# Longitude synthesis moved, by row block, into the prologue of the spiking stage; the spiking weights prepared in the stage of the synthesis over degrees

## The reference

```python
x = x + _L0_conv_ref(_ln_c(x), L0_conv_w1r, L0_conv_w1i, L0_conv_w2r, L0_conv_w2i)   # spherical harmonics: analysis, mixing, synthesis
t = _to_tokens(x)
t = t + _L0_ffn_ref(_ln_t(t))             # decodes nibbles, shifts, adds one-hot rows
x = _from_tokens(t, x)
x = x + _L1_conv_ref(_ln_c(x), ...)       # spiking attention, 8 heads, time axis = batch
t = _to_tokens(x)
t = t + _L1_ffn_ref(_ln_t(t), ...)        # two of eight experts for each token
```

```python
def _isht(c):
    g = jnp.einsum('lmj,bclm->bcjm', P_SYN, c) * (1.0 / np.sqrt(TWO_PI))   # over degrees l
    return jnp.fft.irfft(g, n=NLON, axis=-1) * NLON                        # over orders m: "longitude"
```

## Time and profile before

| | us |
|---|---|
| median of 3 runs | 1368.16 (1367.49 to 1375.95) |
| the profiled execution | 1366.96 |
| its span, first to last instruction | 1364.5 |
| synthesis block | 203.1 to 283.5 |
| weights' block | 283.5 to 299.1 |
| prologue, to the first projection | 299.1 to 334.5 |
| spiking loop, from its first sign | 345.8 to 877.4 |
| experts | from 877.4 |

### The profile page before, as it was taken

How to read it: one execution, slowest core, us unless ns; L and a number is a source line. 1 busy time by engine, 2 the same in 40 slices (tenths; PEclk the granted TensorE clock), 3 DMA queues, 4 the chain that set the end, 5 groups by cost and what they waited for, 6 DMA issues and landing times. The chain is left out here.

```text
span 1364.5 us, 23969 instructions
## 1 busy us (share of the span) xinstructions
PE 993.5 (73%) x6628; PEld 845.5 (62%) x6629; DVE 857.8 (63%) x2741; ACT 655.1 (48%) x1400; POOL 573.4 (42%) x739
## 2 busy tenths in 40 slices
PE   7937665931577767676776754129999999999997
PEld 6827663721355556565565543028888888888886
DVE  6715432454557889889878454616666666666675
ACT  3427532207385887777865342114444444444443
POOL 3310000212022257566655477645555555555554
PEclk9978887875777888797867655559999999999999
DMA  9998949910001001000000000011111111111110
GB/s 277 201 236 157 210 104 261 240 43 20 19 20 49 20 19 41 15 24 23 11 26 15 28 25 27 21 51 45 42 43 46 48 48 48 45 47 48 46 37 1
DMA packets 122841, 93.08 MB, mean 68 GB/s; under 512 B 10760, under 2 KB 111476, under 8 KB 122001
## 3 DMA queue, kind: packets, MB, share of 16 engines
q1 hardware_dynamic: 103121, 66.48, 21.6%
q0 software_dynamic: 9088, 17.33, 3.9%
q10 hardware_dynamic: 10560, 8.39, 2.3%
HBM read 55.61 MB, written 38.39 MB: 69 GB/s over the span
## 5 line engine op out<-in xcount | busy, mean ns | idle before, releaser
L1663 POOL DMA_INDIRECT out_dram<-res,index x156 | 155.8, 999 | 217.7 <-DVE res L1746 192.4
L1793 ACT ACTIVATE sil<-ps_h 128x512 f32<-128x512 f32 x156 | 93.1, 597 | 254.6 <-PE ps_h L1845 254.6
L1711 DVE TENSOR_TENSOR act_rows<-ps_h,sil 128x512 f32<-128x512 f32 x156 | 108.0, 692 | 132.9 <-ACT sil L1793 132.8
L1864 PE MATMUL ps_y<-r_raw,aT 128*128 x1248 | 164.9, 275 | 0.0
L153 POOL DMA_INDIRECT slots<-x_sb,r_pos x128 | 130.9, 1023 | 54.0 <-issue 33.0
L1864 PEld LDWEIGHTS ps_y<-r_raw,aT 128*128 128x128 f32 x1248 | 151.7, 192 | 0.1
L1843 PE MATMUL ps_h<-wp,uTh 128*128 x312 | 137.5, 441 | 1.9 <-DVE uTl L1705 1.6
L1844 PE MATMUL ps_h<-wp,uTh 128*128 x312 | 124.4, 399 | 0.0
L1845 PE MATMUL ps_h<-wp,uTl 128*128 x312 | 122.8, 394 | 0.0
L1070 PE MATMUL ps_q<-wqkv,zT 128*128 128x256 f32 x256 | 114.5, 540 | 0.0
L1182 POOL TENSOR_TENSOR x_sb<-x_sb,sy 128x256 f32<-128x256 f32 x64 | 43.9, 687 | 145.6 <-ACT sy L1318 145.4
(11 more groups left out here) (233 smaller groups left out, 2482.8 us busy)
## 6 DMA issues: line engine op xcount, KB each, us to landing
slots<-zero SPq DMA_DIRECT2D x4, 2652.0 KB, 26.2
pay<-slots SPq DMA_DIRECT2D x39, 272.0 KB, 2.8
wc<-in_L_conv_w1r SPq DMA_DIRECT2D x8, 512.0 KB, 11.4
wc<-in_L_conv_w1i SPq DMA_DIRECT2D x8, 512.0 KB, 11.8
wc<-in_L_conv_w2r SPq DMA_DIRECT2D x8, 512.0 KB, 11.7
wc<-in_L_conv_w2i SPq DMA_DIRECT2D x8, 512.0 KB, 11.7
coefficients<-c ACTq DMA_DIRECT2D x4, 1024.0 KB, 8.6
coefc<-coefficients ACTq DMA_DIRECT2D x16, 256.0 KB, 6.1
```

What stands on the lines that cost most here:

```text
L1663: nc.gpsimd.indirect_dma_start(out_rows, bass.IndirectOffsetOnAxis(at, 0), res[:, m % RES, :], None, bounds_check=TOKENS - 1, oob_is_err=F ...
L1711: nc.vector.tensor_tensor(act_rows[:, k], ps_h[:, k, :, DFF:], sil[:, k], ALU.mult).then_inc(s_act, 1)
L1793: nc.scalar.activation(sil[:, k], ps_h[:, k, :, 0:DFF], ACT.Silu).then_inc(s_sil, 1)
L1864: ins = nc.tensor.matmul(dst, aT[:, k, (2 * e + h) * P:(2 * e + h + 1) * P], raw[:, 4 + h, col], start=(h == 0), stop=(h == 1))
```

## The change

The block of the longitude synthesis is gone. The synthesis over degrees stays in a block, which also does the work of the weights' block: the loads `lw` and `par` are issued behind `psyn` and ahead of `einv` and `gin`, PE turns the weights ahead of its 32 products, and DVE prepares the weights ahead of its 8 copies. The result goes to `routing.orders`, which lies in the memory that the experts' weights take later, so these are loaded only once all of it is turned (`sp.wait_ge(s_ct, 2 * NP2)`).

The longitude synthesis runs in the spiking stage's block, by row block instead of by batch: PE starts with 8 times (8 transposes, 8 products), ACT's copies and DVE's additions stand between the pieces of the prologue, and POOL's copies `hc` are dropped. The products go to two banks, `ps_o` and `ps_y`, in turn (before: four), and DVE frees each by one addition of 512 columns. The statistics of row block i wait for its additions. In ACT's program the scalings of row block 1 move from the prologue to behind the first signs, and of `z` only the first quarter stands ahead of the first projection.

```diff
@@ -142,9 +142,10 @@
     def allocate(self, sb):
 
         self.pos = sb("r_pos", [P, NTILES], U32)
-        self.raw = sb("r_raw", [P, 6, E * C])
+        kept = sb("r_raw", [P, 10, E * C])
+        self.raw, self.last = kept[:, 0:6], kept[0:C - 1, 6:10]
+        self.orders = kept[:, 0:8].rearrange("p a f -> p (a f)").rearrange("p (b h r m) -> p b h r m", b=B, h=HP, r=2)
         self.bias = sb("r_bias", [P, E * C])
-        self.last = sb("r_last_channel", [C - 1, 4, E * C])
 
     def scatter(self, nc, slots, x_sb, w, q):
 
...
-                with pe.Fori(0, B // 2) as pair:
-                    for k in range(2):
-                        b = pair * 2 + k
-
-                        def transposes(g):
-                            pe.wait_ge(s_hT, b * 2 + g + 1)
-                            for q in range(G):
-                                t0 = (g * G + q) * 2
-                                ins = nc.tensor.transpose(ps_t[:, g % 2, q * P:(q + 1) * P],
-                                                          hc[:, k, t0:t0 + 2].rearrange("p q r m -> p (q r m)"), ident[:, :])
-                            ins.then_inc(s_tr, 1)
-
-                        def grid(g):
-                            pe.wait_ge(s_hT, b * 2 + g + 3)
-                            pe.wait_ge(s_yfree, b * 2 + g + 1)
-                            for q in range(G):
-                                ins = nc.tensor.matmul(ps_y[:, g, q], hT[:, g, q * P:(q + 1) * P], einv[:, :],
-                                                       start=True, stop=True)
-                            ins.then_inc(s_y, 1)
-
-                        pe.wait_ge(s_hc, b + 1)
-                        transposes(0)
-                        transposes(1)
-                        grid(0)
-                        grid(1)
-
...
-                        pool.wait_ge(s_tr, b * 2 + 1)
-                        nc.gpsimd.tensor_copy(hc[:, k], h_sb[:, b]).then_inc(s_hc, 1)
...
-                            dve.wait_ge(s_y, n + 3)
-                            for bank in range(2):
-                                rows = x_sb[:, bass.ds(n * 2 * G + bank * G, G), 0:C]
-                                ins = nc.vector.tensor_tensor(
-                                    rows, rows, ps_y[:, g, bank * 2:bank * 2 + 2].rearrange("p q (j c) -> p (q j) c", j=2), ALU.add)
-                            ins.then_inc(s_yfree, 1)
...
         with nc.Block() as block:
             @block.sync
             def _(sp):
+                sp.dma_start(psyn[:, :, :], t["legendre_synthesis"].rearrange("p (m q) -> p m q", m=M)).then_inc(s_psyn, 16)
                 sp.dma_start(lw[:, :, :], t["L1_conv_lin_w"].rearrange("i d c -> d i c")).then_inc(s_load, 16)
                 for n, name in enumerate(("lin_b", "bn_g", "bn_b", "bn_m", "bn_v")):
                     with nc.allow_non_contiguous_dma(reason="512 parameters, once"):
                         sp.dma_start(par[:, n, :], t[f"L1_conv_{name}"].rearrange("i d -> d i")).then_inc(s_load, 16)
+                sp.dma_start(einv[:, :], t["fourier_inverse"]).then_inc(s_einv, 16)
+                for j in range(4):
+                    for op in range(2):
+                        for half in range(2):
+                            src = mixed[op].rearrange("l (j h r) f -> j h l (r f)", j=4, h=2)[j, half]
+                            p0 = op * 64 + half * L2
+                            sp.dma_start(gin[p0:p0 + L2, j].rearrange("p r m o -> p (r m o)"), src).then_inc(s_gin[j], 16)
+                sp.wait_ge(routing.s_zero, 2)
+                part = SLOT_TILES // 4
+                for n in range(4):
+                    sp.dma_start(slots.rearrange("(q p) c -> p q c", p=P)[:, n * part:(n + 1) * part, :],
+                                 routing.zero[:, :].unsqueeze(1).broadcast_to([P, part, XW])).then_inc(routing.s_clear, 16)
...
@@ -713,6 +617,15 @@
                 nc.vector.tensor_copy(wqkv[:, :], ps_w[:, 0:3 * C])
                 nc.vector.tensor_copy(bias[0:3, :], ps_b[:, :])
                 split3(nc, chain, [wo[:, n, :] for n in range(3)], ps_w[:, 3 * C:4 * C], rest[:, :])
+                for n2 in range(1, M // 2, 2):
+                    dve.wait_ge(s_leg, n2 + 1)
+                    evacuate(nc.vector.tensor_copy, n2).then_inc(s_h[1], 1)
+
+            @block.scalar
+            def _(act):
+                for n2 in range(0, M // 2, 2):
+                    act.wait_ge(s_leg, n2 + 1)
+                    evacuate(lambda o, i: nc.scalar.activation(o, i, ACT.Copy), n2).then_inc(s_h[0], 1)
 
...
@@ -722,13 +635,25 @@
                 for i in range(4):
                     ins = nc.tensor.transpose(ps_b[:, i * C:(i + 1) * C], bpart[:, i, :], ident[:, :])
                 ins.then_inc(s_t, 1)
-    return wqkv, wo, bias, ones
+                pe.wait_ge(s_psyn, 16)
+                for n in range(M):
+                    j, at = n // (M // 4), n % (M // 4)
+                    if at == 0:
+                        pe.wait_ge(s_gin[j], 16 * 4)
+                    if n % 2 == 0 and n >= 4:
+                        pe.wait_ge(s_h[(n // 2) % 2], n // 4)
+                    ins = nc.tensor.matmul(ps_g[:, (n // 2) % 2, n % 2, :], psyn[:, at * 4 + j, :],
+                                           gin[:, j, :, at, :], start=True, stop=True)
+                    if n % 2:
+                        ins.then_inc(s_leg, 1)
+    return wqkv, wo, bias, ones, einv, s_einv
...
+        def grid_bank(u):
+            return (ps_o if u % 2 == 0 else ps_y)[:, :]
...
+        def orders_turned(pe, i, g):
+
+            need(pe, s_chT, (i - 1) * 2 + g + 1)
+            for q in range(G):
+                ins = nc.tensor.transpose(ps_kv[:, g, q * P:(q + 1) * P],
+                                          h_sb[:, g * G + q, 2 * i:2 * i + 2].rearrange("p h r m -> p (h r m)"), ident[:, :])
+            ins.then_inc(s_ct, 1)
+
+        def orders_copied(act, i, g):
+
+            act.wait_ge(s_ct, i * 2 + g + 1)
+            need(act, s_cg, ((i - 1) * 2 + g) * 2 + 2)
+            nc.scalar.activation(hT[:, g, :], ps_kv[:, g, :], ACT.Copy).then_inc(s_chT, 1)
+
+        def grid(pe, i, g):
+
+            pe.wait_ge(s_chT, i * 2 + g + 1)
+            for h in range(2):
+                u = (i * 2 + g) * 2 + h
+                need(pe, s_ca, u - 1)
+                for q in range(2):
+                    at = (h * 2 + q) * P
+                    ins = nc.tensor.matmul(grid_bank(u)[:, q * 2 * C:(q + 1) * 2 * C], hT[:, g, at:at + P], einv[:, :],
+                                           start=True, stop=True)
+                ins.then_inc(s_cg, 1)
+
+        def grid_added(dve, i):
+
+            for n in range(4):
+                u = i * 4 + n
+                dve.wait_ge(s_cg, u + 1)
+                rows = xv[:, 2 * n:2 * n + 2, i]
+                nc.vector.tensor_tensor(rows, rows, grid_bank(u).rearrange("p (b j c) -> p b j c", b=2, j=2), ALU.add).then_inc(s_ca, 1)
+
         def statistics(dve, n):
 
             need(dve, s_xu, n)
+            dve.wait_ge(s_ca, n * 4 + 4)
             chain = Chain(dve, s_schain, n * LN_LINKS)
             layer_norm_stats(nc, chain, st, tmp[:, 0], tile(n), NT, 1e-5, -1.0).then_inc(s_var, 1)
...
@@ -1330,6 +1298,7 @@
                 sp.dma_start(before_f[:, :], t["token_before"]).then_inc(s_const, 16)
                 sp.dma_start(routing.bias[:, :], t["L1_ffn_b2"].rearrange("(a e) c -> a (e c)", a=1).broadcast_to([P, E * C]))\
                     .then_inc(routing.s_bias, 16)
+                sp.wait_ge(s_ct, 2 * NP2)
                 for k in range(4):
                     sp.dma_start(routing.raw[0:C - 1, k, :].rearrange("p (e f) -> p e f", e=E),
...
@@ -1346,7 +1315,9 @@
 
             @block.vector
             def _(dve):
+                grid_added(dve, 0)
                 statistics(dve, 0)
+                grid_added(dve, 1)
                 nc.vector.memset(every[:, :], 1.0)
                 nc.vector.memset(chosen[:, :, :], 0.0)
                 nc.vector.memset(fill[:, :], 0.0)
@@ -1359,11 +1330,17 @@
                 dve.wait_ge(s_const, 128)
                 nc.vector.tensor_copy(before[:, :], before_f[:, :]).then_inc(s_set, 1)
                 dve.wait_ge(s_set, 1)
+                grid_added(dve, 2)
+                grid_added(dve, 3)
                 ffn_flags(dve, 0)
+                grid_added(dve, 4)
                 ffn_value(dve, 0)
                 ffn_shift(dve, 0)
+                grid_added(dve, 5)
+                grid_added(dve, 6)
                 ffn_add(dve, 0)
                 z_statistics(dve, 0)
+                grid_added(dve, 7)
                 statistics(dve, 1)
 
                 def beside(i, b):
@@ -1455,13 +1432,27 @@
 
             @block.scalar
             def _(act):
-                u_rows(act, 0, 0, NT)
-                x_rows(act, 0, 0, NT)
-                for g in range(G):
+                def copied(i):
+
+                    for g in range(2):
```

(45 more changed lines are left out.)

108 lines of the change are left out of this document (17 added, 91 removed).

## The result

Before took 1368.5 us (median of 20 runs, 1358.7 to 1385.5), the changed kernel 1348.8 us (20 runs, 1338.1 to 1364.8). The ratio is 0.9841, with a 95% interval of 0.9814 to 0.9869: 21.8 us of 1368.5. Some executions of either kernel are over 1.5% slower than its fastest; the medians are over all runs, the ratios leave these out.

A forecast was written before the change was run, and what follows sets the result against it. Bound: the dependent chain to the loop's first sign, and SP's clearing issue holding the barrier. Sign 20.9 us earlier, 2.0 given back: 1366.96 - 18.9 = 1348.1, with 1.2 for the median 1349 us; range 1343 to 1355.

The forecast's parts named there:

- The barrier, 55.7 us behind `psyn`: End of the merged stage over degrees: SP's clearing issued at 258.6, spiking stage starts at 258.9 us instead of 299.1.
- the third rival: Stage over degrees: SP does not hold the barrier, so it ends at 242.7, 16 us earlier: 1333 us; chance 0.06.
- The first block added after 9.5 us: Start of the merged prologue: cold PE takes 1.97 us for transposes and 6.10 for products, then copies and last addition.
- The chain through DVE from there to POOL's start on the z statistics, 42.2 us: Merged prologue: statistics, row blocks, cast, flags, value and shift in turn on DVE, from 9.5 to 51.7 us.
- The tail, 12.0 us: Prologue's end: POOL 3.6, z rows 1.6, PE's turn 1.1, `zT` 0.6, hand-overs 0.9, projection 4.2; sign at 63.7 us.
- The allowance of 2.3 us for a dip of the clock: Merged prologue: PE's clock could drop between steps while waiting for DVE; half a block's slowdown added, giving 66 us.
- 2.0 us back in the first steps: Behind the first sign: ACT's moved rows hidden in the first step, lengthening the next two by 0.95 us each.
- `before_f` covered by 2.7 us: Spiking stage's constants: landing at 274.6 us behind the clearing, while DVE asks for them at 277.3.
- The second rival: Spiking stage's constants come late, 26.2 us from issue to landing; DVE waits 11.3 us: 1360 us; chance 0.09.
- Loop and experts as long as before; `r_raw` free: Behind the prologue: loop and experts keep their length; `r_raw`, loaded from about 305 us, isn't needed before 877: zero cost.
- The fourth rival: Spiking loop: steps fall to PE's lower clock, a mean of 0.65 costing 47.7 us: 1397 us; chance 0.06.
- the first rival: Merged prologue: PE stays at the lower clock, blocks about 9 us each, sign at 80: 1363 us; chance 0.15.

The follow-up runs named there:

- the first profile: First profile of the unedited changed kernel: 56.9 us for its first two windows together, 62.6 us to the first sign, 532.6 us to the experts' weights.
- late clearing: Changed kernel with the four clearing DMAs of `slots` issued behind the spiking stage's small constants: 1339.5 us, ratio to before 0.9720.
- the repeat: The changed kernel once more, with no edit, beside the kernel before on the same chip: 1345.0 us, ratio to before 0.9817.
- late clearing and four banks: Changed kernel with `slots` clearing behind the spiking stage's constants and products going round four PSUM banks instead of two: 1325.3 us, ratio to before 0.9636.

## Why the prediction was right

It forecast 1349 us and a gain of 18.9; the median gave 1348.8, and 19.7 against the median of before. By the stretches the gain was 25.0 us (22.9 in the first profile), by the ratio 21.8. The mechanism is as forecast, but that the median met the forecast to 0.2 us is luck: the gain was forecast 3 to 6 us too small, and the runs of one kernel lie up to 27 us apart. The terms, in the words of its steps:

- *The barrier, 55.7 us behind `psyn`*: 56.7. Here the argument that was worth most: read from the engines alone (copies at an end after 39.3 us, forecast 39.5; products 18.8 us behind `psyn`, forecast 18.3), the gain would have been 16 us larger, the third rival's 1333. The late clearing then took just that, 17.5 us. One detail was wrong, "the issue is no limit": the six loads push the start of the clearing back by 8.3 us, not 2.3 (17.2 us behind `psyn` instead of 8.9), 4.9 us of it since `bn_m` stands in the full queue, the rest their own issues. But the clearing then takes 39.1 us to issue instead of 44.2, and SP is done 3.1 us later than before. This fits an issue that is paced by the delivery of what stands ahead and not by its own start, though no run sets the two apart.
- *The first block added after 9.5 us*: 7.4 (264.38 to 271.81). I had put PE at the lower clock for all 16 product records. It was so for the first 3.6 us.
- *The chain through DVE from there to POOL's start on the z statistics, 42.2 us*: 42.3. Piece by piece (forecast in brackets): statistics 4.2 (4.3), block 1 3.9 (3.6), memsets and cast 0.9 (1.3), blocks 2 and 3 10.2 (9.8), flags 3.1 (3.1), block 4 3.4 (3.6), value and shift 2.6 (2.7), blocks 5 and 6 8.5 (8.5), addition and statistics 5.4 (5.3).
- *The tail, 12.0 us*: 11.6. It ends with ACT's other 12 z rows (4.71 us), not with PE's projection.
- *The allowance of 2.3 us for a dip of the clock*: the dip behind the first pause costs PE 1.8 us (1.44, 1.91 and 1.57 where it took 1.03, 1.04 and 1.10), of which blocks 1 to 3 show 0.7, inside their terms above. The one behind the last pause is off the chain, since the sign waits for ACT. So nothing stands against the allowance itself, and with it the prologue was mis-sized by 4.7 us: 61.3 instead of 66 (62.6 in the first profile).
- *2.0 us back in the first steps*: 0.6 in the repeat, 2.0 in the first profile of the same kernel, 1.6 in the mean of nine. Steps two and three got longer as forecast; the first got shorter by 1.3 us in the repeat, where PE was at the higher clock in it, and by 0.2 in the first profile, where it was not. The fourth sign came 14.4 and 15.9 us behind the first, forecast 16.
- *`before_f` covered by 2.7 us*: by 0.3. It landed 15.8 us behind the barrier, forecast 15.7; DVE came for it 2.2 us sooner than forecast, with the first block. It held, barely. The second rival's price, 26 us from issue to landing, did not come (3.8), but its point was right that the constants stand behind the clearing; they do so at their issue.
- *Loop and experts as long as before; `r_raw` free*: 1018.3 against 1018.7 us; `r_raw` was issued at 308.9 us without effect. The fourth rival did not come.

Together, for the repeat: 4.7 us of the prologue, 2.4 behind the first sign (0.4 shorter, forecast 2.0 longer), less 1.0 at the barrier, are 6.1 us more than the 18.9, which makes the 25.0. Of the profile's signs for the first rival, PEclk in the prologue was 0.86, with 1.00 from 268 us to the pause, and the blocks cost 3.4 to 5.1 us, not 9. The Trainium skill ("TensorE: Matmul & The Clock Gate", section "A second HAM failure mode: psum-queue depth-cycling") was closer than I gave it credit for, and smaller: the swing that it describes for small waits between groups is there behind the wait of 2.7 us in four of six profiles with two banks, and behind the last one of 3.6 us in all six; behind those of 1.5 and 0.95 us it is in none. Behind the wait of 2.7 us it costs PE 1.5 to 3.2 us, where the rival had 14 for the prologue.

What stays open: whether the ratio of the changed kernel is nearer to 0.984 or 0.982, and why the loop's 64 steps take 427.0 us in one run and 429.7 in another of the same kernel (late clearing and four banks), and whether the late clearing lengthens them.

## What to carry to other kernels

A queue of transfers that an engine issues in a block belongs to that block's length. When a stage is made shorter, read when the issuing engine is done, not only the engines that compute; a transfer that nobody needs soon goes behind those that are needed, and behind the barrier. And when a producer fills banks for a consumer that has other work too, give it as many as it can fill in the meantime: two more banks took the prologue here from 61.3 to 54.2 us.

## What was not expected of the hardware

- The issue of a transfer costs what the queue ahead makes it: `rank` took 0.35 us with an empty queue and 9.06 behind the clearing, `bn_m` 0.51 and 5.37. The Trainium skill ("DMA: Bandwidth & Descriptors", section "Issuing engines are not separate DMA queues") says that the sequencer's time to start a DMA is usually small beside the transfer. An estimate by that rule has SP done some 19 us behind the issue of `psyn` (17.2 to the clearing, and four issues of 0.4 as for the small transfers); measured were 56.2. Here issuing the clearing's 10.6 MB took 39.1 us, and the measurement decides.
- The same instruction after the same pause, 2.69 us, ran at either level of TensorE's clock in two runs of one kernel, 1.10 and 2.05 us for four product records.
